# Linear bias attention of a twelve-part decoder: scratch laid out with heads innermost, fetches of three blocks at a time, a new order of the transfers, and the last projection one slot later

## The reference, cut to what matters

```python
def _L3_attn_ref(x, W_attn, b_attn, W_proj, b_proj, temperature):
    B, T, C = (2, 512, 256)
    H = 16
    D = C // H
    qkv = x @ W_attn + b_attn
    q, k, v = jnp.split(qkv, 3, axis=-1)
    ...
    att = jnp.einsum('bqhd,bkhd->bhqk', q, k) * (1.0 / math.sqrt(D))
    att = att / temperature
    bias = slopes[:, None, None] * (pos[None, :] - pos[:, None])
    att = att + jnp.where(causal, bias, -jnp.inf)
    w = jax.nn.softmax(att, axis=-1)
    y = jnp.einsum('bhqk,bkhd->bqhd', w, v).reshape(Bc, Tc, Cc)
    return y @ W_proj + b_proj
```

## Time and profile before

| what | us |
|---|---|
| median of 3 runs | 1914.26 |
| the 3 runs | 1913.52, 1914.26, 1921.05 |
| the profiled execution | 1920.53 |
| its span | 1919.2 |
| the stage l3_attn in it | 1398 to 1580 |

### The profile page before, as it was taken

The page is one execution under the profiler, slowest core; times in us unless marked ns, Lnnn a source line. Parts: engine busy times, 40 slices in busy tenths (PEclk is TensorE's granted clock), DMA queues, the critical chain, the costliest instruction groups (busy, mean ns, idle before and its releaser), DMA issues. The chain is left out here.

```text
span 1919.2 us, 22974 instructions
## 1 busy us (share of the span) xinstructions
PE 1679.7 (88%) x7761; PEld 862.1 (45%) x7761; DVE 1052.6 (55%) x2139; ACT 905.6 (47%) x1762; POOL 429.9 (22%) x537
## 2 busy tenths in 40 slices
PE   7899997888998689999796899999875986899997
PEld 3334443334664244443344555656332433455545
DVE  4631024493224568888735788887345614545525
ACT  2321204342333267777634777887321643355523
POOL 0000000000000245555301455555010111223210
PEclk9999998999999999999998999999985999899999
DMA  5000100001000000000024111010149001000000
GB/s 212 1 0 0 39 1 1 33 1 44 1 1 17 0 17 9 9 17 23 26 96 165 48 53 37 30 36 30 40 80 156 3 14 68 11 20 20 1 1 23
DMA packets 30564, 66.27 MB, mean 35 GB/s; under 512 B 4469, under 2 KB 15541, under 8 KB 29013
## 3 DMA queue, kind: packets, MB, share of 16 engines
q1 hardware_dynamic: 30448, 64.81, 11.5%
HBM read 55.78 MB, written 8.91 MB: 34 GB/s over the span
## 5 line engine op out<-in xcount | busy, mean ns | idle before, releaser
L2247 POOL TENSOR_TENSOR work<-work,arena_a 128x512 f32<-128x512 f32 x128 | 167.5, 1309 | 153.1 <-ACT work L2112 152.9
L1986 PE MATMUL ps<-identity,ctx_keys 128*128 128x128 f32 x1024 | 144.9, 281 | 17.0 <-ACT work L2112 14.5
L2201 DVE CUSTOM_DVE_ANT_0 ctx_keys<-ps,arena_b 128x1024 f32<-128x1024 f32 x128 | 154.9, 1212 | 6.7 <-ACT arena_b L2063 6.5
L1986 PEld LDWEIGHTS ps<-identity,ctx_keys 128*128 128x128 f32 x1024 | 118.6, 144 | 64.8 <-ACT work L2112 21.1
L2094 ACT ACTIVATE ctx_keys<-ctx_keys,small 128x1024 f32<-128x1024 f32 x128 | 146.9, 1147 | 0.7 <-DVE small L2201 0.7
L2213 DVE TENSOR_TENSOR work<-ps,arena_a 128x512 f32<-128x512 f32 x128 | 88.0, 688 | 44.1 <-PE ps L1986 40.0
L3064 POOL TENSOR_SCALAR ctx_keys<-ctx_keys,small 128x128 f32<-128x128 f32 (+3 forms) x128 | 66.4, 531 | 178.0 <-DVE small L3013 170.7
L2112 ACT ACTIVATE work<-ps 128x512 f32<-128x512 f32 x128 | 76.3, 596 | 62.4 <-PE ps L1986 59.2
L338 PE MATMUL ps<-work,arena_a 128*128 128x512 f32 x192 | 85.1, 595 | 7.9 <-DVE work L512 3.2
L1788 POOL TENSOR_SCALAR work<-work 128x1024 f32<-128x1024 int32 x64 | 66.6, 1040 | 112.7 <-DVE work L1741 112.2
L2960 ACT ACTIVATE ctx_keys<-ctx_keys,small 128x128 f32<-128x128 f32 (+3 forms) x128 | 70.8, 554 | 39.5 <-DVE small L3000 39.0
(11 more groups left out here) (386 smaller groups left out, 3466.8 us busy)
## 6 DMA issues: line engine op xcount, KB each, us to landing
arena_b<-in_mask SPq DMA_DIRECT2D x2, 2048.0 KB, 8.6
arena_a<-in_groupT SPq DMA_DIRECT2D x2, 2048.0 KB, 14.6
head_weights<-in_w_L_xattn SPq DMA_DIRECT2D x8, 449.0 KB, 3.2
arena_a<-in_w_l_attn SPq DMA_DIRECT2D x1, 3072.0 KB, 14.7
head_weights<-in_w_L_attn SPq DMA_DIRECT2D x8, 384.0 KB, 3.1
work<-parts_q_L_attn SPq DMA_DIRECT2D x24, 128.0 KB, 10.9
work<-parts_k_L_attn SPq DMA_DIRECT2D x24, 128.0 KB, 13.0
work<-parts_k_L_xattn SPq DMA_DIRECT2D x15, 192.0 KB
```

Of the source, the lines that this page charges most:

```text
L1986: mm = pe.transpose(t_psum[z][:, kt * P:(kt + 1) * P], prob[i % NP][:, o:o + P], k.iden[:, :])
L2201: dve.tensor_tensor_reduce(prob[i % NP], s_psum[i % NS], NEG[:, b, qt, :], -1.0, BIG * 3e8, OP.add, OP.min, minmax[:, i % 8:i % 8 + 1]).th ...
L2247: pool.tensor_tensor(p, p, GT[:, b, 4:8, qt * P:(qt + 1) * P], OP.mult).then_inc(*weighed_pool.up())
```

## The change

The scratch tensors are indexed feature, piece, head, token, so the four heads of a group are one run of 8 KB. A fetch of a group is 6 transfers instead of 12: for q pieces 0 to 2 into 48 partitions, 0 and 1 into 32, 0 into 16; for k the same piece repeated 3, 2 and 1 times. The order of SyncE's list becomes: ..., group 1, wait for all stores, then for each pair p its rows of maxima, with group 2 after pair 0, group 3 after pair 1 and the next stage's weights after pair 2. TensorE gets 12 matmuls on the identity (`beat`) ahead of the first slot and one in each of the slots 0 to 7. The last part of the first half's projection moves from u == 30 to u == 31, and the last normalisation goes from GpSimd to VectorE (signal `scaled`).

```diff
-    scr = {n: k.nc.dram_tensor(f"parts_{n}_{name}", (H, dh, 3, NT), BF16, kind="Internal").ap() for n in "qk"}
-    PARTS = {"q": (0, 1, 2, 0, 1, 0), "k": (0, 0, 0, 1, 1, 2)}
+    scr = {n: k.nc.dram_tensor(f"parts_{n}_{name}", (dh, 3, H, NT), BF16, kind="Internal").ap() for n in "qk"}
+    PIECES = {"q": (range(0, 3), range(0, 2), range(0, 1)), "k": ((0, 0, 0), (1, 1), (2,))}
...
-            sp.dma_start(scr[which][8 * m:8 * m + 8, :, :, t0:t0 + S].rearrange("h f j t -> (h f) j t"),
+            sp.dma_start(scr[which][:, :, 8 * m:8 * m + 8, t0:t0 + S].rearrange("f j h t -> h f j t"),
                          parts[x]).then_inc(*stored.up())
             if x == NC // 2 - 1:
                 sp.wait_ge(*stored(x + 1))
                 fetch(sp, 0)
         fetch(sp, 1)
         sp.wait_ge(*stored(NC))
-        fetch(sp, 2)
-        sp.wait_ge(*values(nk))
-        l3_xattn_loads(k, sp)
         for p in range(H // 2):
...
-            if p == 0:
-                fetch(sp, 3)
+            if p < 2:
+                fetch(sp, 2 + p)
+            if p == 2:
+                sp.wait_ge(*values(nk))
+                l3_xattn_loads(k, sp)
 
     def fetch(sp, g):
         for which in "qk":
-            for blk, j in enumerate(PARTS[which]):
-                sp.dma_start(stack[which][BIAS + dh * blk:BIAS + dh * blk + dh, 4 * g:4 * g + 4],
-                             scr[which][4 * g:4 * g + 4, :, j].rearrange("h f t -> f h t")).then_inc(*fetched[g].up())
+            row = BIAS
+            for block in PIECES[which]:
+                n, j = len(block), block[0]
+                src = scr[which][:, 0:n, 4 * g:4 * g + 4, :] if which == "q" else scr[which][:, j:j + 1, 4 * g:4 * g + 4,
+                                                                                              :].broadcast_to([dh, n, 4, NT])
+                sp.dma_start(stack[which][row:row + dh * n, 4 * g:4 * g + 4], src.rearrange("f j h t -> j f (h t)")).then_inc(
+                    *fetched[g].up())
+                row += dh * n
...
+        k.beat(o_bank, 12)
...
-                    pe.wait_ge(*fetched[s // 8](12))
+                    pe.wait_ge(*fetched[s // 8](6))
...
+                if s < LAG - 2:
+                    k.beat(o_bank, 1)
...
-            if u == 30:
+            if u == 31:
                 pe.wait_ge(*put(7))
...
-        pe.wait_ge(*put(8))
+        pe.wait_ge(*scaled(1))
...
+        dve.wait_ge(*inverse(8))
+        dve.tensor_tensor(O[7], U[1], R, OP.mult).then_inc(*scaled.up())
         absorb(dve, 1)
...
-        normalise(pool, 7)
```

More of the change, by code:

```diff
@@ L2450, in l3_attn @@
     k_plain, hi, top_out, top_hi, exped, gathered, logged, inverse = k.signals("act", 8)
-    q_plain, rest1, low, tempered, values, maxed, top_rest, top_low, resid = k.signals("dve", 9)
+    q_plain, rest1, low, tempered, values, maxed, top_rest, top_low, resid, scaled = k.signals("dve", 10)
     middle, cleared, top_mid, put = k.signals("pool", 4)
```

## The result

The change takes 1953.89 us (4 runs, 1952.41 to 1964.31) against 1917.53 us, ratio 1.0202, 95% interval 1.0158 to 1.0246. The forecast was 1943 us in 1926 to 1962, slower. Its profiled execution has a span of 1953.4 us against 1919.2.

The account below looks back on a forecast made before the run. The stage was taken to run at the pace of a first-in-first-out transfer queue, set by its fullest DMA engine. Slot 18's +31.9 less 3.6 at the end gave +28.3 us on the median 1914.26, rounded to 1943, range 1926 to 1962.

Parts of the forecast that it names:

- Width 3 and 2, always the lowest engines: Group fetches: transfers with outermost index 3 or 2 run on only 3 or 2 DMA engines, always starting at engine 0.
- 21.5 us per group: Fetch of a group: engine 0 is busy 21.5 us instead of 11.0, between ends of 20.3 and 25.1.
- Stores at 2.3 us: Stores to the scratch: each runs on 8 engines with 49 packets, taking 2.3 us instead of 1.15.
- 21.5 more: Upper end for the stores: at 5.5 us each they would add 21.5 us to the sum; held unlikely.
- Slot 18 at +31.9: TensorE at slot 18: waits for pair 2's rows of maxima until 1529.3 against 1497.38, so 31.9 us later.
- Order of need: SyncE's new list order: removes the 12 us wait at slot 10, but the slower groups give back more.
- Tail -3.6: End of the stage: moved projection saves 1.9 and 1.1 us, normalisation on VectorE 0.6; ends -2.5 and -3.6.
- The median as a base: Final sum: +28.3 us, taken from one profiled execution of 1920.53 us, is added to the median of 1914.26.
- Rival (a): Group fetches use their partitions' full width: a group takes 3.7 us at 425 GB/s, kernel 1889 us; chance 0.07.
- The 7.2 us that the prediction estimates from ports: Group fetch under the full-width rival: 7.2 us if bandwidth follows the ports reached, 8 for 48 partitions; sum about 1890.
- Rival (b): Rows of maxima pass the groups in the queue, so only groups bound: +16.0 - 3.6, 1927 us; chance 0.08.
- Rival (c): Nearly no change: transfers of 3 and 2 use different engines, the new order's gain cancels the rest, near 1914; chance 0.06.

Follow-up runs that it names:

- wide: The change with the fetch sources permuted so that their outermost index is the 16 features, rows of the stack reordered alike: 1901.96 us, ratio 0.9912 to the kernel before.
- narrow: The kernel before with the new scratch and the 6 new transfers per group, in the old order, without beats, with the old ending: 1977.84 us, ratio 1.0304.
- eight: The kernel before with one unused row between the heads of the scratch, so a store's outermost index is 8, rows still 2 KB apart: 1930.54 us, ratio 1.0082.
- tail: The kernel before with only the last projection at u == 31 and the last normalisation on VectorE: 1913.73 us, ratio 0.9979.
- again: The change itself measured in a second set of runs against the kernel before: 1956.49 us, ratio 1.0222.
- spread: The kernel before with the 16 rows of each transfer written 6 partitions apart, same 12 transfers, scratch and order: 1909.08 us, ratio 0.9966.

## Why the prediction was right, and what was mis-sized

The direction, the mechanism and the range held; the rise was 36 to 42 us by the medians, the forecast 28.

- **Width 3 and 2, always the lowest engines**: right. 664 fewer small packets, as those widths give, 2.9 engines busy, and `wide`.
- **21.5 us per group**: 21.9 from slot 12's rows to slot 18's, 22.4 from slot 8 to slot 12. The inner value was right. Group 0 took 26.7 us from issue to slot 0 against 23.7: +3.0. But from slot 0 to slot 8, four stores and group 1, it took 29.5 against 30.7: -1.2. The two stretches belong together: in `narrow` they are 25.0 and 30.9, and the sum is 55.9 where the change has 56.2. So it looks as if store packets were served while group 0 still ran; the sum alone shows a loss, 1.8 us, and no run isolates it.
- **Stores at 2.3 us**: wrong in size. Two of them delay group 0 by 4.15 us, not 2.3. The step was "a store runs on 8 engines, 49 packets, 2.3 us": the width was right (`eight`), the 46 ns per packet became 58. +1.85. The upper end's "21.5 more" is also a slip: stores of 5.5 us, two ahead of group 0 and four behind it, would add 6 x 3.2 = 19.2 to the sum.
- **Slot 18 at +31.9**: +36.6, counted from the first store. The sum was short by 4.7: +1.85 from stores 2 and 3, +1.8 from issue of group 0 to slot 8, and +0.6 and +0.4 for groups 2 and 3, at 22.4 and 21.9 us.
- **Order of need**: right in both senses, the wait at slot 10 gone, and pairs 1 and 2 each behind a group, 14.62 and 6.38 us (forecast over 10, and 5.9).
- **Tail -3.6**: from the product with v at u = 28 to the next stage's mean 25.55 us before, 21.61 after: -3.9, though the last projection still waits 2.1 us, not under 2. From slot 18 to that product it takes 57.3 us before and 58.3 after: slot 18 restarts at a clock of 0.50 (its first matmuls take 0.93 us, not 0.54), which the sum lacked, +1.0. With slot 18's +36.6, 36.6 + 1.0 - 3.9 = 33.7, the stage's growth.
- **The median as a base**: the sum came from one execution, 3.0 us over the median of its kernel, with some 3 us of waits more than `tail` had for the same transfers. Against a typical before the change may cost that much more: 36 to 37 with the stage's 33.7, where 36.4 was measured. That is argued, not shown. The clock ahead of the stage's first store (-3.0) and behind the stage (+2.8) happened to cancel in the two profiles, and such shifts are of the size of what is left open, some 5 us of the 41.6 of `again`.
- **Rival (a)** fell with the packets, but its reason, that something other than the engines' own rate limits a transfer into 16 partitions, was right: `spread`. Its price was not: with full width (`wide`) a group takes about 9 us, not 3.7, and the kernel 1902, not 1889 (slow stores included, which that rival left out). The 7.2 us that the prediction estimates from ports is nearer. **Rival (b)** fell with the waits of 14.6 and 6.4 us for rows of maxima. **Rival (c)** fell with the ratio of 1.0202.

## What to carry to other kernels

Before a transfer is reshaped, write down the size of the outermost index on both sides: with 3, 2 or 8 there it ran on 3, 2 or 8 engines here, and one permutation of the source was worth 52 us. Count the small packets of a stretch: here they were the completion writes, one per engine used. In a queue that is worked off in order, price the fullest engine, not the bytes. And where rows needn't be neighbours, try writing them apart, and price the longer issue.

## What was not expected of the hardware

- With stores on 8 engines it takes 6.9 us in place of 2.8 us from the fourth store's issue to group 0's, more than half the width explains: a packet took 58 ns in place of 47.
- Transfers into 16 neighbouring partitions: 131 to 163 GB/s with all engines shown as full, whatever the run length; into 48 neighbouring ones 176; into 48 every second one 252 to 266.
- Issuing a transfer whose partitions are 6 apart took SyncE 0.63 to 0.68 us, one of 16 neighbours 0.45.
- One of SyncE's issues stood for 14.34 us while the lowest engines had much queued, though only about 3 of the 16 worked for much of it (share 0.18 in 1442 to 1450).
- The same 77 matmuls behind the stage took 20.2 us at a granted clock of 1.00 and 29.8 us at 0.69, in kernels that don't differ there.
